# State product of a Mamba-2 layer in three fp32r passes, and the skip product folded into the y addition

## What is computed

```
proj = einsum('bld,pd->blp', hidden, in_proj_w)      # gate (4096), x, B and C (6144), dt (64)
xBC  = silu(causal conv of 4 taps over x, B, C)
dt   = softplus(dt + dt_bias);  dA = exp(-exp(A_log) * dt)
state = state * dA + (dt * x) outer B                # 64 heads of 64, 128 states
y     = state . C + x * D                            # D: one number per head
yn    = y * rsqrt(mean(y*y) over 512 + eps) * norm_weight * silu(gate)
out   = einsum('bli,di->bld', yn, out_proj_w)
```

## Time and profile before

| | |
|---|---|
| median of 3 runs | 1791.78 us (1790.74 to 1792.49) |
| the profiled execution | 1791.13 us, its span 1789.3 us |
| TensorE busy, granted clock | 98%, 1.00 |
| VectorE, GpSimd, ScalarE busy | 85%, 64%, 47% |

### The profile page before, as it was taken

The page is one execution under the profiler, slowest core; times in us unless marked ns, Lnnn a source line. Parts: engine busy times, 40 slices in busy tenths (PEclk is TensorE's granted clock), DMA queues, the critical chain, the costliest instruction groups (busy, mean ns, idle before and its releaser), DMA issues.

```text
span 1789.3 us, 30683 instructions
## 1 busy us (share of the span) xinstructions
PE 1757.7 (98%) x11416; PEld 1416.3 (79%) x11416; DVE 1523.1 (85%) x1936; ACT 836.0 (47%) x1923; POOL 1145.7 (64%) x1143
## 2 busy tenths in 40 slices
PE   8999999999999999999999999999999999999997
PEld 5777888888888888888778788888888888888875
DVE  7879888898988889888888988889898888989887
ACT  4564453544445353443534444354443445444465
POOL 6447466475756657575697847658474764857567
PEclk9999999999999999999999999999999999999999
DMA  8533333232333323233574423333233332324234
GB/s 266 159 126 118 118 114 123 95 119 95 118 119 105 131 95 118 95 113 132 168 230 136 138 101 122 106 104 128 78 125 111 123 114 95 123 90 130 95 112 148
DMA packets 113508, 220.78 MB, mean 123 GB/s; under 512 B 10448, under 2 KB 46672, under 8 KB 113360
## 3 DMA queue, kind: packets, MB, share of 16 engines
q1 hardware_dynamic: 112320, 218.66, 36.8%
q10 hardware_dynamic: 1040, 0.16, 0.1%
HBM read 204.63 MB, written 14.16 MB: 122 GB/s over the span
## 4 chain that ended last, share of the span: by engine, by line
PE 83%; DVE 8%; ACT 4%; issue 2%; POOL 2%; DMA 1%; SPq 0%; ACTq 0%; DVEq 0%; POOLq 0%
PE ps_conv L1307 9%; PE ps_conv L1310 9%; PE ps_y L1486 6%; PE ps_conv L1313 6%; PE ps_out L1307 6%; PE ps_out L1310 6%; PE ps_gate L1307 6%; PE ps_gate L1310 6%; PE ps_y L1491 5%; PE ps_s L1523 5%; PE ps_out L1313 4%; PE ps_gate L1313 4%; PE turned_x L1403 3%; DVE xc L888 2%; PE ps_conv L1314 2%
## 5 line engine op out<-in xcount | busy, mean ns | idle before, releaser
L888 DVE SCALAR_TENSOR_TENSOR xc<-ps_conv,convw_sb,xc 128x511 f32<-128x511 f32 (+2 forms) x576 | 430.5, 747 | 154.0 <-ACT xc L654 140.5
L1240 POOL TENSOR_TENSOR rstd_col<-mean_square,half 128x1 f32<-128x1 f32 x128 | 88.8, 693 | 534.3 <-ACT mean_square L797 534.3
L1012 DVE TENSOR_TENSOR_SCAN decay<-decay,eye 128x1024 f32<-128x1024 f32 x125 | 294.3, 2354 | 0.0
L660 ACT ACTIVATE xc<-xc 128x512 f32<-128x512 f32 x192 | 121.1, 632 | 322.2 <-DVE xc L888 320.6
L1229 POOL TENSOR_TENSOR cpre<-cpre,xc 128x1024 f32<-128x1024 f32 x112 | 268.7, 2399 | 0.0
L1307 PE MATMUL ps_conv<-xn_hi,wconv_hi 128*128 128x512 f32 x768 | 241.9, 437 | 0.0
L1310 PE MATMUL ps_conv<-xn_hi,wconv_lo 128*128 128x512 f32 x768 | 207.4, 392 | 0.0
L1486 PE MATMUL ps_y<-decay,dtx 128*64 128x128 f32 x1984 | 190.9, 279 | 3.6 <-DVE decay L1033 2.8
L1307 PEld LDWEIGHTS ps_conv<-xn_hi,wconv_hi 128*128 128x128 f32 x768 | 141.4, 194 | 49.3 <-issue 27.4
L806 ACT ACTIVATE square<-ps_y 128x512 f32<-128x512 f32 x126 | 75.6, 600 | 219.0 <-DVE ps_y L1065 219.0
L1491 PE MATMUL ps_y<-cpre,state 128*64 128x128 f32 x1760 | 171.3, 273 | 0.0
(11 more groups left out here) (250 smaller groups left out, 3861.6 us busy)
## 6 DMA issues: line engine op xcount, KB each, us to landing
decay<-decays_d SPq DMA_DIRECT2D x125, 512.0 KB, 5.3
cpre<-rows_d SPq DMA_DIRECT2D x112, 512.0 KB, 4.0
stage<-w_in_t SPq DMA_DIRECT2D x32, 1024.0 KB, 6.6
stage<-w_out_t SPq DMA_DIRECT2D x16, 1024.0 KB, 5.5
stage<-w_in_t SPq DMA_DIRECT2D x32, 256.0 KB, 3.2
out_sum<-hidden SPq DMA_DIRECT2D x16, 256.0 KB, 5.7
ffn_d<-sgate SPq DMA_DIRECT2D x16, 256.0 KB, 3.2
out<-out_sum SPq DMA_DIRECT2D x16, 256.0 KB, 3.3
```

Of the source, the lines that this page charges most:

```text
L888: e.scalar_tensor_tensor(acc[:, d:], ps[:, 0:BLK - d], convw_sb[:, tile, TAPS - 1 - d:TAPS - d], acc[:, d:], ALU.mult, ALU.add).then_inc(S ...
L1012: e.tensor_tensor_scan(d, d, eye8[:, :, :].rearrange("p h i -> p (h i)"), 0.0, ALU.mult, ALU.add).then_inc(scanned(i)[0], 1)
```

## The change

The state product of 98 chunks is made in three fp32r passes. For these ScalarE makes b_hi and xw_hi by copies, GpSimd makes b_lo and xw_lo by subtractions; TensorE's passes are b_hi x xw_hi, b_lo x xw_hi, b_hi x xw_lo. The other 14 of the 112 (steps 58 to 62, 64, 65 and those from 120 on) stay in fp32. For the chunks before 120 the skip tile goes: VectorE forms x * D + y in four operations, one for each 128 channels, since D is then one number per partition. GpSimd's order changes: one output weight tile before xw_lo and three after cpre, the convolution and most gate splits behind cpre or at the end of a step. The buffer for GpSimd-made DMA descriptors is set to 1024 bytes; the kernel makes none.

```diff
+def split_state(i):
+
+    return i < SCALED_XW and i % NCH < NCH - 1 and finished(i) is None
+
+
+def split(i):
+
+    return sum(split_state(k) for k in range(i + 1))
...
+        xw_hi = sb("xw_hi", [P, GC], F32R)
+        xw_lo = sb("xw_lo", [P, GC], F32R)
...
+        b_hi = sb("b_hi", [P, NS], F32R)
+        b_lo = sb("b_lo", [P, NS], F32R)
...
-                    w.wait_ge(S["skip"], CPB * (nb - 1))
+                    w.wait_ge(S["y"], CPB * (nb - 1))
...
+                    if split_state(i):
+                        e.activation(b_hi[:, :], ps_g[:, 0:P], ACT.Copy)
                     e.activation(b_tok[:, :], ps_g[:, 0:P], ACT.Copy).then_inc(S["b_tok"], 1)
...
+                if split_state(i):
+                    w.wait_ge(S["xw"], inner(i))
+                    w.wait_ge(S["mm_u"], inner(i) - 1)
+                    e.activation(xw_hi[:, :], xw[:, :], ACT.Copy).then_inc(S["xw_hi"], 1)
...
                     w.wait_ge(S["mm_in"], m + 1)
-                    w.wait_ge(S["skip"], m + 1)
-                    e.tensor_tensor(y_bank(m)[:, :], y_bank(m)[:, :], skip[:, :], ALU.add).then_inc(S["y"], 1)
+                    if m < SCALED_XW:
+                        w.wait_ge(S["silu"], max(conv_no(m // CPB, t) for t in range(XT)) + 1)
+                        w.wait_ge(S["par"], 128)
+                        for t in range(XT):
+                            tile = group(m) % GROUPS * XT + t
+                            y_t = y_bank(m)[:, t * P:(t + 1) * P]
+                            done = e.scalar_tensor_tensor(y_t, xc[m // CPB % 2][:, t, block_cols(m % NCH)],
+                                                          dskip_sb[:, tile:tile + 1], y_t, ALU.mult, ALU.add)
+                        done.then_inc(S["y"], 1)
+                    else:
+                        w.wait_ge(S["skip"], m - SCALED_XW + 1)
+                        e.tensor_tensor(y_bank(m)[:, :], y_bank(m)[:, :], skip[:, :], ALU.add).then_inc(S["y"], 1)
...
-                if i < N:
-                    g, at = divmod(i, NCH)
-                    left = BATCH * GROUPS - 1 - g
-                    if at == 1:
-                        if g == 0:
-                            w.wait_ge(S["last"], inner(i))
-                        split_out(g, range(XT))
-                    if at == 3 and left:
-                        split_conv_x(g + 1, range(KT))
-                    if at == 4 and left:
-                        split_gate(g + 1, (0, 1))
-                    if at == 5 and left:
-                        split_conv_bc(g + 1, range(KT))
-                    if at == 6 and left:
-                        split_gate(g + 1, (2, 3))
-                if i < N and i % NCH > 0:
+                g, at = divmod(i, NCH)
+                if split_state(i):
+                    w.wait_ge(S["b_tok"], inner(i))
+                    e.tensor_tensor(b_lo[:, :], b_tok[:, :], b_hi[:, :].bitcast(F32), ALU.subtract).then_inc(S["b_lo"], 1)
+                left = i < N and BATCH * GROUPS - 1 - g
+                if i < N and at == 1:
+                    if g == 0:
+                        w.wait_ge(S["last"], inner(i))
+                    split_out(g, (0,))
+                if split_state(i):
+                    w.wait_ge(S["xw_hi"], split(i))
+                    e.tensor_tensor(xw_lo[:, :], xw[:, :], xw_hi[:, :].bitcast(F32), ALU.subtract).then_inc(S["xw_lo"], 1)
+                if i < N and at > 0:
                     left_of_state(i)
+                if i < N and at == 1:
+                    split_out(g, (1, 2, 3))
+                if at == 4 and left:
+                    split_gate(g + 1, (0,))
+                if at == 5 and left:
+                    split_conv_bc(g + 1, range(KT))
+                if at == 6 and left:
+                    split_gate(g + 1, (2, 3))
...
+                if at == 5 and left:
+                    split_gate(g + 1, (1,))
+                if SCALED_XW <= i < N:
...
+                if at == 2 and left:
+                    split_conv_x(g + 1, (0, 1, 2))
+                if at == 3 and left:
+                    split_conv_x(g + 1, (3,))
...
-                    w.wait_ge(S["b_tok"], inner(i))
-                    w.wait_ge(S["xw"], inner(i))
                     w.wait_ge(S["state"], inner(m) if m >= 0 else 0)
-                    e.matmul(ps_s[:, :], b_tok[:, :], xw[:, :], start=True, stop=True).then_inc(S["mm_u"], 1)
+                    if split_state(i):
+                        w.wait_ge(S["b_tok"], inner(i))
+                        w.wait_ge(S["xw_hi"], split(i))
+                        e.matmul(ps_s[:, :], b_hi[:, :], xw_hi[:, :], start=True, stop=False)
+                        w.wait_ge(S["b_lo"], split(i))
+                        e.matmul(ps_s[:, :], b_lo[:, :], xw_hi[:, :], start=False, stop=False)
+                        w.wait_ge(S["xw_lo"], split(i))
+                        e.matmul(ps_s[:, :], b_hi[:, :], xw_lo[:, :], start=False, stop=True).then_inc(S["mm_u"], 1)
+                    else:
+                        w.wait_ge(S["b_tok"], inner(i))
+                        w.wait_ge(S["xw"], inner(i))
+                        e.matmul(ps_s[:, :], b_tok[:, :], xw[:, :], start=True, stop=True).then_inc(S["mm_u"], 1)
```

More of the change, by code:

```diff
@@ L241, in build @@
             landed_rows0 landed_rows1 st_rows10 st_rows11 st_rows00 st_rows01
-            mm_t dtx scan last xw mm_bt b_tok mm_g M skip cpre mm_gate sgate mm_in mm_u
+            mm_t dtx scan last xw xw_hi xw_lo mm_bt b_tok b_lo mm_g M skip cpre mm_gate sgate mm_in mm_u
             y state sdec square sum1 sum2 mm_ssq var2 rstd2 yg hi2 lo2 mm_out osum
@@ L1264, in _ @@
                     e.tensor_tensor(square_sum[:, :], square[:, 0:P], square[:, P:2 * P], ALU.add).then_inc(S["sum2"], 1)
+                if 0 <= m < N:
+                    bm, cm, gm = batch(m), m % NCH, group(m) % GROUPS
                     if cm < NCH - 2:
@@ L1559 @@
     }
-    nc = bacc.Bacc("TRN2", target_bir_lowering=False, num_devices=1)
+    nc = bacc.Bacc("TRN2", target_bir_lowering=False, num_devices=1, dynamic_dma_scratch_size=1024)
     args = [nc.dram_tensor(name, a.shape, mybir.dt.from_np(a.dtype), kind="ExternalInput").ap()
```

1 line of the change is left out of this document (removed).

## The result

The changed kernel takes 1800.18 us (median of 4 runs, 1798.9 to 1801.64) beside 1791.26 us for the kernel before on the same chip: ratio 1.0052, 95% interval 1.004 to 1.0064. It is slower by 9 us; the forecast was 1800.4 us.

A forecast was written before the change was run, and what follows sets the result against it. Bound: TensorE, with VectorE and ScalarE's path 0.52 us behind. Fourteen groups at +0.70 us give +9.8, plus 0.5 and 0.3, less 2 for output steps: +8.6, so 1800.4 us median; range 1792 to 1808.

The forecast's parts named there:

- What bounds the kernel: TensorE 98% busy, but VectorE and ScalarE's path through four y additions to position 3's mixing matrix has only 0.52 us slack.
- d: Extra VectorE time per y addition when four pieces replace one operation: 0.44 us taken, bounds 0.06 to 0.71.
- The price of the pieces: VectorE's y addition: 351 ns per piece, 1.13 us for four overlapping pieces, against 689 ns for one operation.
- rival 3: VectorE's pieces do not overlap, costing 0.71 us extra per addition: +24 us, 1815.8 us; chance 0.12.
- The gain per product: TensorE saves 0.18 us per split state product, 17.6 us for 98; positions 4 to 6 keep 0.54 a group.
- GpSimd in position 1: TensorE's third state pass waits about 0.4 us for xw_lo, beside the longer path; the moved splits cost nothing.
- the sign that the prediction named: TensorE entering position 4 waits about 1.2 us more for the mixing matrix in every group.
- the path stays hidden: Rival: pieces cheap enough that TensorE keeps its gains, 1777 us, or 1774 without position 1's wait; chance 0.24.
- The lost skip tile: GpSimd's 1.04 us less per step gives back perhaps 2 us in steps 58 to 65; VectorE busy 53 us more.
- rival 4: GpSimd's moved splits and decayed state collide with VectorE's scan after position 1: up to 0.37 us per group, +5 us.
- The ends: Beyond fourteen groups' +9.8 us: unsplit products in group 7 +0.5, group 0 +0.3, group 15 nothing, output steps perhaps -2.
- P: The prediction's theory: the VectorE and ScalarE path through four y additions decides the time, not GpSimd's longer work.

The follow-up runs named there:

- e2: Changed kernel with every state product back in fp32, y still in four pieces: 1806.22 us.
- e4: Changed kernel with y's addition in eight pieces of 64 columns instead of four of 128: 1830.87 us.
- e7: Changed kernel with GpSimd's order eased and edges early, four pieces only for chunks 7, 0, 1, 2 of a group, skip tiles for the others: 1799.22 us.
- e3: Changed kernel with y's addition as one operation over 512 columns, using the first tile's D for all four tiles: 1788.74 us.
- e1: Changed kernel with three-pass state products kept, but y again one tensor_tensor with GpSimd's skip tile in all chunks: 1800.66 us.
- e6: Changed kernel with GpSimd's order eased and edges early, four pieces only for chunks 3 to 6 of a group, skip tiles for the others: 1793.56 us.
- e10: Changed kernel with ScalarE's scalings moved to position 7, GpSimd's order eased, edges early, and skip tiles in all chunks instead of pieces: 1782.99 us.
- e8: Changed kernel with ScalarE's scaling of four output tiles moved from position 0 to the end of position 7: 1790.19 us.
- e5: Changed kernel with GpSimd's order at position 1 altered: xw_lo first, then all four output tiles, then cpre: 1799.60 us.
- e12: Changed kernel with y as one operation (first tile's D for all four), GpSimd's order eased and edges ahead of xw_lo: 1782.49 us.
- e11: Changed kernel with all pieces kept, ScalarE's scalings moved to position 7, GpSimd's order eased and edges early: 1784.18 us.
- e13: As e11, but with skip tiles and one tensor_tensor for chunks 0 and 2 of each group: 1776.40 us.

## Why the prediction was right, and where it wasn't

*What bounds the kernel.* Right. TensorE at 98% did not mean that its time counts: the path found by following the mixing matrix back is the one that the chain of waits now shows, and e2, e4 and e7 confirm its four additions and its slack of 0.52: TensorE entered position 4 late by 1.14, 3.16 and 1.24 us, where four times d less 0.52 gives 1.20, 3.20 and 1.20.

*The price of the pieces.* Right: 348 ns each (351 worked out), four in 1.12 us (1.13), so d = 0.43 against 0.44. A piece starts 0.26 us after the one before. The Trainium skill's "VectorE: DVE Perf Modes" (The DRAIN you can't avoid), by which the next instruction waits for an empty pipe, would have given 4 x 0.348 = 1.39 us. The same section adds that a next operation which is not held starts earlier, and the prediction left that out; with its 1.12 us the trace agrees with the addition, so by the whole section rival 3 did not hold. The advice in the page's "Rules for kernel authors", fewer operations, holds: e4 pays 0.50 us more for the same columns.

*The gain per product.* Too small: 0.16 to 0.23 us in a position without a wait, not 0.18. Positions 4, 5 and 6 kept 0.16 + 0.23 + 0.23 = 0.62 for 0.54. With 1.29 for 1.24 at the entry into position 4 the group comes to +0.67 for +0.70.

*GpSimd in position 1.* This step failed. The wait for xw_lo was priced at 0.4 us (0.3 to 0.9) and took 0.68 in starts. The output tiles that move behind cpre were costed at nothing: the last three end at 451.4, and TensorE's third output pass, due at about 450.8 (0.91 after the second, which starts at 449.86), starts at 451.47, 0.7 late. I had looked at who waits on SP's queue for the moved splits and not at who reads them on TensorE. So the sign that the prediction named, some 1.2 us more of waiting for the mixing matrix at position 4, did not show: that wait is 0.30 us (0.37 in starts), because position 1 had taken the rest. The prediction of the time stays right only because this delay lies beside the longer path, as it said of the xw_lo wait; with the pieces cheap it would have been the bound, and the rival "the path stays hidden" would have given 1789 us (e3) and not 1777. (Its other figure, 1774 without that wait, is a slip: 98 x 0.18 and the 2 us of steps 58 to 65 make 1772.)

*The lost skip tile.* It was counted as a small relief in steps 58 to 65 alone, and VectorE was forecast to be busy 53 us more. It was busy 33 us more. The additions themselves grew by 134.3 + 4.2 (six tensor_tensors left) - 86.8 = 51.7 us; but the scans fell from 294.3 to 287.0 us and `last` from 31.9 to 21.1. Two meetings of every group are gone. In position 5 of the kernel before, the skip tile was running when the scan started (2.65 us). In position 4 it was the squares' sum, and the decayed state, started in that scan, held up `last`:

```profile
474.59 2.45 DVE L1012 TENSOR_TENSOR_SCAN decay<-decay,eye 128x1024 f32<-128x1024 f32 x1
477.07 0.82 DVE L1019 TENSOR_TENSOR last<-decay,prefix_dt 128x8 f32<-128x8 f32 x1
```

```profile
474.85 3.02 POOL L1276 TENSOR_TENSOR state<-state,total_bc 128x512 f32<-128x512 f32 x1
```

Both lay beside the path. e1, e6 and e10 show what the skip tile costs on it. The meeting (rival 4) did not come as feared: in groups 1 to 6 and 9 to 13 of the changed kernel the scans take 2.28 us in every position.

*The ends.* Groups 1 to 6 and 9 to 13 grew by 7.4 us together (11 x 0.7 forecast), group 14 by 1.0, groups 7 and 8 shrank by 1.0 (0.1 forecast), and group 0 grew by 2.35 us where 0.3 was forecast. The misses of 2.0 and 0.9 have opposite signs, and the base moved too: the forecast added 8.6 to a median of 1791.78, while the traces differ by 9.5 and the kernel before measured 1791.26 beside the changed one. So part of the agreement to 0.2 us is luck.

*Group 0.* Timeline of the changed kernel: GpSimd's last edge, ScalarE's first tap that waits for it, TensorE's wait; then the stretches that follow (busy us by engine, the granted clock before the last two figures).

```profile
117.13 0.21 POOL L1197 TENSOR_TENSOR edge<-edge_in,edge 128x6 f32<-128x6 f32 x1
```

```profile
117.45 0.84 ACT L667 ACTIVATE xc<-ps_conv,edge,convw_sb 128x1 f32<-128x1 f32 x3 [0.70 <-POOL edge L1197]
```

```profile
126.71 0.50 PE L1566 MATMUL ps_s<-xw_hi,b_hi 128*128 128x512 f32 x1 [2.88 <-DVE state L1104]
```

```profile
124.00:126.00 2.00, 0.00 (x0) 0.00 (x0) 1.93 (x8) 1.01 (x4) 1.54 (x2) 1.00 0.00 0
...
128.00:131.00 3.00, 3.00 (x8) 2.33 (x8) 2.32 (x4) 1.07 (x3) 3.00 (x3) 0.50 0.00 0
```

xw_lo stands ahead of the edges; the first tap comes 1.5 us later than before, TensorE runs out of work, and the clock falls to half. TensorE waits 2.0 us longer than before (2.88 for 0.87), and its next eight convolution passes take 1.5 us more; by the end of the group its lateness is down to 2.35.

*My expectations.* Three misses have one root each. e1 and e3: P took 0.9 to 1.0 us for GpSimd's waits in position 1, where e3 lost 1.29 and e1 1.93 (its figure in the table and the 0.23 not gained), and it left out what the returning skip tile does to the path. e6: that tile was priced by its mean of 1040 ns, not by what it meets. e8: I took it that a path shortened at one place is shorter by that much; it only begins at the next thing that is late.

## What to carry over

An engine at 98% is a bound only as long as nothing else is within the gain: look for the shortest slack of every chain that hands work to it, those of the helper engines too, before counting what is taken off it. For each instruction that a change moves, ask who reads it next, on which pass, and not just what is queued behind it. Where two paths lie close together, taking away the shorter shows nothing (e5), the longer only a part (e3), and both show the whole (e12): an experiment with both is what tells two paths from a wrong theory. An edit that takes work off one engine by giving it to another (e1) changes both paths at once.

## What the runs showed of the chip that I had not expected

**GpSimd and VectorE's scan block each other, both ways.** A GpSimd tensor_tensor with its tiles in SBUF that starts while VectorE's scan runs lasts until after the scan: 3.02 us for 1.04 (512 columns), 1.67 for 0.55 (one column). The 27 skip tiles of e1 that started in a scan all ended 0.83 to 0.84 us after it. A scan that starts while such an operation runs takes longer by what is left of it, less some 0.13 us: 2.68 for 2.28, started at 447.89 with the decayed state running to 448.42. The Trainium skill's "SBUF — State Buffer" (Who interferes with whom) describes this as a lock on a shared pair of ports, held for the whole instruction by whoever comes first, and names VectorE operations with two SBUF inputs; these rows agree. What it costs depends on the step: in e10 the skip tile of chunk 1 took 3.02 us, that of chunk 2 1.05.

**The clock fell within a short pause.** In group 0 of the changed kernel TensorE had no matmul from 124 to 126 us, and the stretch 128 to 131 was granted 0.50, the level of 1.2 GHz; four convolution passes took 1.71 us in the chain of waits for 0.91 else. In e11, with a wait of 2.07 us at the same place and 0.57 us of work in 124 to 126, the clock stayed at 1.00, and so it did in the kernel before, where the wait was 0.87 us. But the length of that wait alone does not decide: it was 1.64 us in the trace of e6 and 2.08 in that of e7, and the stretch 126 to 128 was granted 0.58 and 0.63, while in e10 (1.63) and e13 (1.65) the clock stayed at 1.00. What else decides is open. The clock fell there in eight of the 14 traces, which moves one time against another by some 1.5 us; the table leaves group 0 out, so its intervals are free of it.
